# A graph attention layer: the clearing of the gather buffer and the diagonal's presence move to VectorE, late attentions move to every third block

## What is computed

```python
feats = (X @ W).reshape(-1, H, D)                      # H = D = 8
a_self  = einsum('nhd,hd->nh', feats, att_self)
a_neigh = einsum('nhd,hd->nh', feats, att_neigh)
scores = a_self.T[:, :, None] + a_neigh.T[:, None, :]
scores = leaky_relu(scores, 0.2) + (-1e10 * (1.0 - A))[None, :, :]
attn = softmax(scores, axis=-1)
out = einsum('hij,jhd->ihd', attn, feats) + bias
x = layernorm(x + relu(out.reshape(-1, H * D)))
```

## Time and profile before

| | |
|---|---|
| runs | 843.20, 844.21, 846.03 us (median 844.21) |
| the profiled execution | 844.56 us, its span 842.7 us |
| busy, share of the span | PE 600.1 us (71%), DVE 587.8 us (70%), POOL 502.0 us (60%), ACT 78.2 us (9%) |
| DMA | 291.79 MB, 346 GB/s over the span |
| the last `adj` quarter's matmuls | begin at 746.48 us |

### The profile page before, as it was taken

The page is one execution under the profiler, slowest core; times in us unless marked ns, Lnnn a source line. Parts: engine busy times, 40 slices in busy tenths (PEclk is TensorE's granted clock), DMA queues, the critical chain, the costliest instruction groups (busy, mean ns, idle before and its releaser), DMA issues.

```text
span 842.7 us, 8722 instructions
## 1 busy us (share of the span) xinstructions
PE 600.1 (71%) x2132; PEld 289.6 (34%) x2133; DVE 587.8 (70%) x1683; ACT 78.2 (9%) x355; POOL 502.0 (60%) x464
## 2 busy tenths in 40 slices
PE   2766665588669797868888786976769685835564
PEld 1621111146314352433424251533335141504343
DVE  5567994641796878676666675677668977847885
ACT  1200000210010101000001000011020110102010
POOL 4100977777607777777777777766464757636400
PEclk9885555558979988886868695989799696958787
DMA  7999999999999999999999999999999999931100
GB/s 284 363 413 389 408 391 345 329 359 398 399 419 404 398 399 397 401 396 399 398 399 399 398 398 398 397 400 396 373 369 408 399 406 397 403 136 27 37 1 25
DMA packets 76230, 291.79 MB, mean 346 GB/s; under 512 B 31318, under 2 KB 39307, under 8 KB 43408
## 3 DMA queue, kind: packets, MB, share of 16 engines
q1 hardware_dynamic: 56784, 275.44, 83.4%
q0 software_dynamic: 14208, 10.46, 4.3%
q10 hardware_dynamic: 5184, 5.31, 1.9%
HBM read 294.39 MB, written 4.75 MB: 355 GB/s over the span
## 4 chain that ended last, share of the span: by engine, by line
DMA 52%; PE 27%; DVE 13%; issue 5%; SPq 1%; ACT 1%; DVEq 0%; ACTq 0%
DMA adj_sb<-in_adj_dram 51%; PE xt_ps L676 13%; PE codes L648 11%; DVE spare L926 2%; DVE head_mask L792 1%; PE ft_ps L633 1%; PE xt_ps L678 1%; PE ft_ps L717 1%; SPq L402 1%; DVE top L912 1%; DMA base<-in_L_gnn_att_self_dram 1%; DVE z L903 1%; DVE z L911 1%; DVE z L915 0%; DVE z L906 0%
## 5 line engine op out<-in xcount | busy, mean ns | idle before, releaser
L444 POOL DMA_INDIRECT near<-node_table,idx x444 | 489.6, 1103 | 278.6 <-issue 192.9
L648 PE MATMUL codes<-adj_sb,weights 128*128 128x512 bf16 x1024 | 349.5, 482 | 165.1 <-DMA adj_sb<-in_adj_dram 164.8
L648 PEld LDWEIGHTS codes<-adj_sb,weights 128*128 128x128 bf16 x1024 | 100.6, 109 | 393.7 <-issue 339.2
L676 PE MATMUL xt_ps<-spare,ident 128*128 128x360 f32 (+4 forms) x734 | 195.4, 416 | 29.6 <-DVE spare L926 29.6
L676 PEld LDWEIGHTS xt_ps<-spare,ident 128*128 128x128 f32 x734 | 135.5, 198 | 81.5 <-issue 41.8
L816 DVE MAX8 val<-codes 128x8 f32<-128x128 f32 x192 | 42.7, 284 | 140.7 <-PE codes L648 134.0
L926 DVE TENSOR_TENSOR spare<-near,spare 128x704 f32<-128x704 f32 (+12 forms) x64 | 101.1, 1641 | 9.1 <-ACT spare L571 9.1
L821 DVE MAX8 val<-codes 128x8 f32<-128x64 f32 (+2 forms) x156 | 19.6, 198 | 42.8 <-PE codes L648 42.0
L571 ACT ACTIVATE spare<-z 128x736 f32<-128x736 f32 (+10 forms) x16 | 14.9, 933 | 215.4 <-DVEq L918 215.4
L641 PE MATMUL codes<-place,weights 128*128 128x512 bf16 x64 | 31.3, 490 | 0.0
L872 DVE MAX8 key<-left 128x8 f32<-128x168 f32 (+2 forms) x79 | 28.7, 363 | 2.7
(11 more groups left out here) (156 smaller groups left out, 483.6 us busy)
## 6 DMA issues: line engine op xcount, KB each, us to landing
adj_sb<-in_adj_dram SPq DMA_DIRECT2D x256, 1024.0 KB, 16.7
near<-node_table,idx POOLq DMA_INDIRECT x444, 5.8
node_table<-spare ACTq DMA_DIRECT2D x4, 648.0 KB, 7.9
spare<-in_x_dram SPq DMA_DIRECT2D x4, 512.0 KB, 7.7
self_sb<-node_table ACTq DMA_DIRECT2D x16, 121.5 KB, 7.6
x_sb<-in_x_dram SPq DMA_DIRECT2D x4, 384.0 KB, 18.1
out_dram<-x_sb SPq DMA_DIRECT2D x1, 768.0 KB, 12.6
self_sb<-node_table ACTq DMA_DIRECT2D x16, 40.5 KB, 10.1
```

Source lines behind the costliest of these rows:

```text
L444: pool.indirect_dma_start(out=near[:, near_at(t) + k, :], out_offset=None, in_=table[:, :], in_offset=bass.IndirectOffsetOnAxis(ap=idx[t % ...
L648: last = pe.matmul(codes[i][:, :], weights[:, kk, :], adj_bf[q][:, k * GC:(k + 1) * GC, 1], start=False, stop=(kk == BITS - 1))
L676: last = pe.matmul(to[:, a:b, :], ident[:, :], slot_rows(t, s, a, b), start=(s == 0), stop=(s == W - 1))
```

## The change

Four edits. `ATTEND` is three blocks apart (with single steps of four) from tile 5 on, so that tiles 6 to 15 attend one to three blocks earlier. `near` is cleared by DVE, as its first instruction, and no longer by POOL. The four loads of `diag` are gone. In their place `compact` computes it: keys minus the keys with the rows' own taken out leaves only the own keys that were found; MAX8 collects them (`own_found`), each is compared with the four that belong to the rows (`own_equal`), and a maximum over these gives `diag[:, t, :]`. That is four DVE instructions per tile.

```diff
-    ATTEND = [16, 20, 24, 28, 32, 36, 40, 44, 47, 50, 53, 57, 60, 64, 67, 70]
+    ATTEND = [16, 20, 24, 28, 32, 36, 39, 42, 45, 48, 51, 55, 58, 61, 64, 67]
...
+        own_found = sb("own_found", [P, 8], fp32)
+        own_equal = sb("own_equal", [P, RING, RING], fp32)
...
-                if 9 <= n < 9 + RING:
-                    r = n - 9
-                    of = diag_heads if r == REST else diag_rest[:, :, r]
-                    sp.dma_start(diag[:, :, r], of, allow_slow_non_contiguous=True).then_inc(diag_loaded, 16)
...
-            pool.wait_ge(weights_ready, 1)
-            pool.memset(near[:, :, :], 0.0).then_inc(near_zeroed, 1)
...
+            dve.memset(near[:, :, :], 0.0).then_inc(near_zeroed, 1)
             dve.wait_ge(params_loaded, 64)
...
                 step(dve.match_replace(rest_keys[:, 0:C], self_key[:, t, :], keys[:, 0:C], 0.0))
+                step(dve.tensor_tensor(work[:, 0:C], keys[:, 0:C], rest_keys[:, 0:C], ALU.subtract))
+                step(dve.max(own_found[:, :], work[:, 0:C]))
+                step(dve.tensor_tensor(own_equal[:, :, :], own_found[:, 0:RING].unsqueeze(1).to_broadcast([P, RING, RING]),
+                                       self_key[:, t, 0:RING].unsqueeze(2).to_broadcast([P, RING, RING]), ALU.is_equal))
+                dve.tensor_reduce(diag[:, t, :], own_equal[:, :, :], AX.X, ALU.max)
...
-                    dve.wait_ge(diag_loaded, 16 * RING)
```

More of the change, by code:

```diff
@@ L263, in gat_resnorm @@
         x_loaded = sem("x_loaded")
-        diag_loaded = sem("diag_loaded")
         cols_loaded = [sem(f"cols_loaded{i}") for i in range(XG)]
@@ L373, in _ @@
                 sp.dma_start(x_cols[:, cols, :], x_rows[:, cols, :]).then_inc(cols_loaded[c], 16)
-            on_diagonal = adj.rearrange("r c -> (r c)")[0:N * N:N + 1]
-            diag_heads = on_diagonal[0:NH * P].rearrange("(t p) -> p t", p=P)
-            diag_rest = on_diagonal[NH * P:N].rearrange("(t p j) -> p t j", p=P, j=REST)
             def load_behind(n):
```

## The result

The changed kernel takes 821.52 us (median of 4 runs, 820.76 to 822.09) against 844.8 for the kernel before: ratio 0.9728, 95% interval 0.971 to 0.9747, so 23.0 us less (21.4 to 24.5). In a second session it took 820.89 us, ratio 0.971 (0.9697 to 0.9722). The forecast was 823.2. The profiled execution took 821.55 us, with a span of 819.7; its last codes are taken 6.8 us earlier than before (748.50), and what lies behind them is 16.2 us shorter (819.7 - 741.70 = 78.0, before 842.7 - 748.50 = 94.2). 6.8 + 16.2 = 23.0.

The account below looks back on a forecast made before the run. Bound by DMA loading `adj` at 403 GB/s until about 747 us, then by the DVE, ACT and PE chain for the last tiles. 844.56 - 2 - 9.2 - 14.2 + 4 = 823.2 us, range 813 to 833.

Parts of the forecast that it names:

- The clearing, -2 us: At the start, clearing near on VectorE lets an early load request move up: 2 us less, ends 0.5 and 2.9.
- The low end, 0.5: At the start, from 28 to 44 us: hardly 0.5 us of the lost DMA time was idle.
- The diagonal's loads, -9.2 us: From 133 to 178 us, dropping the 4-byte loads lifts DMA from 321 to 403 GB/s: 9.2 us less, low end 5.
- The presence operations, +1.1 us in the tail: Four added DVE operations per tile: free beside the stream, 1.1 us on tile 15's path behind the last load.
- The tail, -14.2 us: Behind the last load, earlier attentions start tile 15's scores at 791.0, not 805.18; the gather decides; ends 11.0 and 16.8.
- The estimate of 2.1: Landing of the last gather, 41 KB, by the Trainium skill: would make the sum 0.5 us lower.
- the median of 5.8: Landing of all gathers, most beside the stream: for the last gather it would make the sum 3.2 us higher.
- The loop, +4 us: In the stream, PE waits about 5.6 us at block 42, block 50's dip goes: net 4 us more, ends -3.7 and +8.
- the 2 us allowed for tile 7: In the stream, tile 7's weigh follows tile 6's, late by what was lost: 2 us more.
- the ring does not dry again and again: Rival: attentions three blocks apart make quarters late five times; 855.5 us at 8 us each, 5%; weaker form around 834, 10%.
- the dips of the diagonal are not merely moved: Rival: from 133 to 178 us something else holds the buffers, so that term is 0: 832.4 us, 9%.
- the start does not count whole: Rival: the stream hangs on PE's start, 6.3 us in place of 2, no loss around block 42: 811 to 817, 8%.

Follow-up runs that it names:

- late presence: Changed kernel with three of the four presence operations put behind the row numbers that start the gather: 821.31 us, ratio 0.9713.
- later sums: Changed kernel with tile 6's sums four blocks behind its attention instead of three: 822.46 us, ratio 0.9739.
- the two kernels without it: Changed kernel with tile 6's sums a block later, 822.46 us; the same with late presence and early rows added, 818.9 us.
- the clearing alone: Kernel before with only the clearing of near moved from GpSimd to VectorE's start: 844.73 us, ratio 0.9999.
- all three edits: Changed kernel with tile 6's sums a block later, three presence operations behind the row numbers and tile 15's first eight row numbers early: 818.9 us, ratio 0.9685.
- early rows: Changed kernel with tile 15's first eight row numbers written behind the first of four compaction rounds, so its gather starts earlier: 819.28 us, ratio 0.9696.
- presence undone: Changed kernel with the diagonal loaded from the matrix again and no presence operations: 830.21 us, ratio 0.9821.
- weighing left out: Changed kernel without the four long multiplications of tile 14's weighing: 821.46 us, ratio 0.9713.

## Why the prediction was right, point by point

The forecast missed the median by 1.7 us, with errors of its terms that went both ways. That the last codes came within 0.4 us of the place worked out (741.70; 748.50 - 7.2 = 741.3) is luck in part: the clearing's 2 us did not come, and the loop cost about 2 us less than its 4.

- **The clearing, -2 us: failed.** Measured 0.1 us less alone (0.9 less to 0.8 more), nothing in the changed kernel. The step that failed is the bytes from 28 to 44 us, counted as gained for good. They came (370 GB/s alone, 1.5 us at 403) and were given back by 133 us, since loads bound the next stretch. The clearing itself was as worked out, 9.24 us, but began at 3.11 us and not at 0.1, behind an idle time of 2.99 us for which the trace names no releaser; DVE came to the features at 20.59, 3.7 us earlier than before and not 6.3. The low end, 0.5, was nearest.
- **The diagonal's loads, -9.2 us: right in the new order, too much alone.** The stretch went to 397 GB/s: 45 x (397 - 321) / 403 = 8.5 us. Undoing the part in the changed kernel costs 7.9 to 9.4, with the presence operations in it; alone it gives 5.2. The 12.7 us of landing are the median of the four; the first took 20.7.
- **The presence operations, +1.1 us in the tail: their length right, their price not seen.** 0.33, 0.34, 0.17 and 0.17 us, 1.0 in all with the steps between. But moving three of them off the path changed nothing measurable, and without them the tail took 78.1 and 80.0 us, with them 78.0 and 79.1.
- **The tail, -14.2 us: right, the gain 1 to 2 us larger.** 94.2 became 78.0 and 79.1. `idx` was written 10.7 us behind the last codes (10.5 worked out), DVE was ready for the scores 37.1 behind them (782.95 - 4.16 - 741.70; worked out 37.0), and the gather decided, as forecast. The scores started 41.25 and 42.03 behind them, worked out 42.5: the last issue was over 27.9 us after the first began, not 28.4, and the landing passed on 1.63 and 2.47 us later, not 2.6. The estimate of 2.1 from the Trainium skill ("DMA: Bandwidth & Descriptors", Anatomy of one DMA — SWDGE (gpsimd) path) lies between the two; the median of 5.8 does not hold for this idle DMA. From the scores to the end it took 36.8 and 37.1 us, where 37.5 were carried over from before.
- **The loop, +4 us: mechanism right, price too high.** PE's wait at block 42 was 5.23 us (5.6 worked out), the stream's loss 15 x (403 - 275) / 403 = 4.8 us (5.8), the dip at block 50 gone. The term that was too large is the 2 us allowed for tile 7: PE did wait 5.00 us for its weighing, but the stream lost nothing there (399 GB/s from 524 to 560 us). In the last codes the new order costs 0.7 and 2.5 us (749.18 against 748.50, 751.13 against 748.61). The bytes that a dip misses were an upper bound of its price: in the two kernels without it, some 2.6 us of them went at the end of the stream, where the last load landed late all the same.

The rivals: the ring does not dry again and again (alone the attentions give 13.3 us). PE waited for the weighing of tiles 6, 7 and 8 (5.23, 5.00 and 2.79 us), where the prediction had seen a reason for tile 6 alone, but only the first wait shows as a dip. The other two: the dips of the diagonal are not merely moved; the start does not count whole, or at all.

What stays open: why the presence gives more in the new order than in the old, why the last load lands no sooner when the stream has run ahead, and why PE's wait at block 42 dries the stream and the next two don't.

## What to carry to other kernels

A gap in a transfer rate is an upper bound of what an edit there can win: count it only if the next stretch can't make it up, and test the part alone. In a tail that hangs on one gather, find the last issue and its landing, and start the first issues on the first results; what runs on VectorE beside them, and a clock of TensorE that comes back late in the sums behind, can take back about a microsecond each. Errors of several terms can cancel: a total that fits says little about its parts.

## What was not expected of the hardware

GpSimd's issue of an indirect gather took 1.63 us instead of 1.00 beside VectorE's 128x704 multiplications with two inputs, and in the changed kernel's trace up to 2.23, beside tile 13's weighing:

```profile
737.83 2.23 POOL L434 DMA_INDIRECT near<-node_table,idx  x1 [0.31 <-issue]
```

Tile 14's multiplications cost the last gather 1.0 us by the run that left them out, and 2.5 us by the gaps in the traces with the late presence and the later sums.

Tile 15's sums, the same matmuls each time, ran from the first matmul to the next step's in 11.2 to 12.6 us. In every trace the granted clock was 0.50 for the first three microseconds, and 0.62 to 0.97 over the next four. How long TensorE had idled before does not order these times: they took 12.6 us after 6.46 us of idling (the clearing alone), 12.2 after 5.25 (all three edits), 11.2 after 6.64 (early rows), 11.6 after 11.61 (presence undone) and 12.4 after 14.02 (weighing left out). What decides it is open.
